# Mixture-of-experts block: expert outputs scattered into six planes, or added by the DMA into four

## The reference, cut to what matters

```
routing_weights = jax.nn.softmax(xf @ router_weight.T, axis=-1)
_, top_idx = jax.lax.top_k(routing_weights + e_score_bias, 6)
top_w = take(routing_weights, top_idx) / sum
combine = zeros((T, E)).at[arange(T)[:, None], top_idx].add(top_w)
gate, up = split(einsum('th,eih->tei', x, gate_up_proj), 2)
y = einsum('tei,ehi->teh', silu(gate) * up, down_proj)
out = einsum('teh,te->th', y, combine) + shared_out
x = x + gb * out
```

## Time and profile before

| | |
|---|---|
| median of 3 runs | 802.63 us (802.34 to 802.96) |
| span of the profiled execution | 799.6 us |
| time around the span, median less span | 3.0 us |
| expert loop, from the first gate matmul to the last down product | about 358 to 733 us |
| tail, from there to the end of the span | about 66 us |
| DMA traffic | 158.45 MB, 198 GB/s in the mean |

### The profile page before, as it was taken

The page is one execution under the profiler, slowest core; times in us unless marked ns, Lnnn a source line. Parts: engine busy times, 40 slices in busy tenths (PEclk is TensorE's granted clock), DMA queues, the critical chain, the costliest instruction groups (busy, mean ns, idle before and its releaser), DMA issues.

```text
span 799.6 us, 13266 instructions
## 1 busy us (share of the span) xinstructions
PE 740.7 (93%) x4302; PEld 590.7 (74%) x4302; DVE 480.8 (60%) x1207; ACT 400.0 (50%) x943; POOL 411.3 (51%) x420
## 2 busy tenths in 40 slices
PE   4989999999999898969999899999999999999963
PEld 4465667657657555549999799999999999997521
DVE  3676678879869954533555244444544544446986
ACT  5267574874464174115655455555565655662000
POOL 0000000267777777777777766765666666666000
PEclk9996999999999999989999999999999999999997
DMA  9420001024235896556676866765765666677995
GB/s 327 132 80 1 0 1 54 34 107 177 116 123 218 315 393 235 227 196 230 227 255 218 284 219 216 230 220 165 226 202 179 194 204 199 194 265 265 363 413 222
DMA packets 82605, 158.45 MB, mean 198 GB/s; under 512 B 14430, under 2 KB 55523, under 8 KB 82280
## 3 DMA queue, kind: packets, MB, share of 16 engines
q1 hardware_dynamic: 58344, 96.74, 36.9%
q0 software_dynamic: 19968, 56.67, 17.8%
q10 hardware_dynamic: 4224, 4.19, 1.5%
HBM read 88.15 MB, written 73.57 MB: 202 GB/s over the span
## 4 chain that ended last, share of the span: by engine, by line
PE 69%; DVE 9%; POOL 8%; DMA 5%; issue 4%; ACT 3%; SPq 2%; DVEq 0%; ACTq 0%; POOLq 0%
PE ps_wide L1320 17%; PE ps_wide L1335 12%; PE ps_kv L1320 8%; PE ps_wide L1089 8%; POOL expert_rows L541 8%; PE ps_narrow L1308 6%; DMA arena<-expert_outs 2%; PE ps_wide L1082 2%; PE ps_wide L1111 2%; PE ps_kv L1344 2%; PE ps_narrow L1040 1%; PE ps_narrow L1102 1%; PE ps_kv L1111 1%; DMA arena<-expert_rows 1%; DMA arena<-w_g 1%
## 5 line engine op out<-in xcount | busy, mean ns | idle before, releaser
L541 POOL DMA_INDIRECT expert_rows<-arena,slot_i x192 | 193.3, 1007 | 215.7 <-DVE arena L1638 151.2
L647 POOL DMA_INDIRECT expert_outs<-arena,meta x224 | 217.8, 972 | 111.7 <-DVE arena L1842 69.6
L894 ACT COPY arena<-arena 128x512 f32 x224 | 127.4, 616 | 157.0 <-PE ps_narrow L1308 153.4
L1842 DVE TENSOR_SCALAR arena<-ps_wide,meta 128x256 f32<-128x256 f32 x224 | 98.1, 479 | 129.9 <-PE ps_wide L1335 129.4
L1320 PEld LDWEIGHTS ps_wide<-arena 128*128 128x128 f32 x1200 | 148.4, 195 | 4.0 <-issue 0.2
L1320 PE MATMUL ps_wide<-arena 128*128 128x128 f32 x1200 | 149.0, 278 | 0.0
L1335 PE MATMUL ps_wide<-arena 128*128 x448 | 116.1, 382 | 0.9 <-DVE arena L1818 0.5
L1335 PEld LDWEIGHTS ps_wide<-arena 128*128 128x128 f32 x448 | 76.8, 191 | 7.4 <-issue 1.5
L1089 PE MATMUL ps_wide<-arena 128*128 128x512 f32 x168 | 75.4, 597 | 2.8 <-DVE arena L1532 2.8
L1308 PE MATMUL ps_narrow<-cst,arena 128*128 128x128 f32 x448 | 69.2, 277 | 7.9 <-DMA arena<-expert_rows 7.8
L1320 PEld LDWEIGHTS ps_kv<-arena 128*128 128x128 f32 x592 | 71.8, 192 | 1.9
(11 more groups left out here) (235 smaller groups left out, 1012.3 us busy)
## 6 DMA issues: line engine op xcount, KB each, us to landing
arena<-expert_rows SPq DMA_DIRECT2D x224, 160.0 KB, 2.8
arena<-expert_outs SPq DMA_DIRECT2D x48, 512.0 KB, 13.2
arena<-w_experts SPq DMA_DIRECT2D x32, 384.0 KB, 8.3
expert_rows<-pad_row SPq DMA_DIRECT2D x33, 160.0 KB, 5.0
out<-x ACTq DMA_DIRECT2D x8, 512.0 KB, 10.1
expert_outs<-arena,meta POOLq DMA_INDIRECT x224, 3.1
x<-x SPq DMA_DIRECT2D x3, 1024.0 KB, 11.1
h_cols<-arena SPq DMA_DIRECT2D x6, 512.0 KB, 3.8
```

Of the source, the lines that this page charges most:

```text
L541: nc.gpsimd.indirect_dma_start(rows, bass.IndirectOffsetOnAxis(ap=slots_i[b % 2][:, t, k:k + 1], axis=0), hrows[b % 2][:, t, :], None, bou ...
L647: nc.gpsimd.indirect_dma_start(outs, bass.IndirectOffsetOnAxis(ap=meta_i[:, j % METAS, 1:2], axis=0), yb[j % OUTS], None, bounds_check=las ...
L894: last = nc.scalar.copy(wgu[:, j % 4:j % 4 + 1, :], wall[:, bass.ds(expert[j], 1), 0:DOWN])
L1842: v.tensor_scalar(yb[j % OUTS], ps_wide[:, 1, p % 2, j % DUO * D:(j % DUO + 1) * D], meta[:, j % METAS, 0:1], None, ALU.mult).then_inc(s_y ...
```

## The change

`expert_outs` becomes four DRAM tensors (planes) of T + 128 rows. They are zeroed by four DMAs from the zero row early in the kernel. The store of block j adds its 128 rows to plane j % 4 (`compute_op=ALU.add`), and POOL issues it after the store of block j - 4, the one before it in the same plane, has landed. Padding rows now point to the 128 rows behind the T tokens and are stored too. `rows_of_slots` loses its scan; the output row is the token. The tail reads four planes a part into `FIN` = 6 sets, `CLEAR` is 5, PE and DVE share the planes anew, both wait for all four planes of a part, and SP no longer waits for the last (empty) blocks' stores before it loads the remaining parts.

```diff
-OUT_ROWS = TOPK * T
+PLANES = 4
+FIN = 6
+PLANE_ROWS = T + P
...
-FIN = 4
-BY_PE = [[3, 4, 5] if n in (3, 5, 7) else [4, 5] for n in range(8)]
-BY_DVE = [[k for k in range(TOPK) if k not in by_pe] for by_pe in BY_PE]
+BY_DVE = [[0, 1, 2] if n == 0 else [0] if n in (5, 7) else [0, 1] for n in range(8)]
+BY_PE = [[k for k in range(PLANES) if k not in by_dve] for by_dve in BY_DVE]
...
             sp.dma_start(rows[E * REGION:E * REGION + P, :], pad_row[:]).then_inc(s_stored, 16)
+            for q in range(PLANES):
+                sp.dma_start(outs[q].rearrange("(n p) d -> p n d", p=P),
+                             pad_row[:, None, 0:D].to_broadcast([P, PLANE_ROWS // P, D])).then_inc(s_zero, 16)
...
-                for k in BY_PE[n] + BY_DVE[n]:
-                    sp.dma_start(fin[n % FIN][k], outs[k * T + first:k * T + first + PART * P, :].rearrange(
-                        "(p t) d -> p t d", p=P)).then_inc(s_fin_pe[n] if k in BY_PE[n] else s_fin[n], 16)
+                for k in range(PLANES):
+                    sp.dma_start(fin[n % FIN][k], outs[k][first:first + PART * P, :].rearrange(
+                        "(p t) d -> p t d", p=P)).then_inc(s_fin[n], 16)
...
             for n in range(CLEAR):
                 load_planes(n)
-            for u in range(UNROLL):
-                sp.wait_ge(s_put[u], 16 * ROUNDS // LAPS)
             sp.wait_ge(s_y, DUOS)
             for n in range(CLEAR, PARTS):
                 load_planes(n)
+            for u in range(UNROLL):
+                sp.wait_ge(s_put[u], 16 * ROUNDS // LAPS)
...
+            pool.wait_ge(s_zero, 16 * PLANES)
             for j in range(BLOCKS):
                 u = j % UNROLL
+                if j >= PLANES:
+                    old = j - PLANES
+                    pool.wait_ge(s_put[old % UNROLL], (old // UNROLL + 1) * 16)
                 pool.wait_ge(s_yc, j + 1)
-                nc.gpsimd.indirect_dma_start(outs, bass.IndirectOffsetOnAxis(ap=meta_i[:, j % METAS, 1:2], axis=0),
-                                             yb[j % OUTS], None, bounds_check=last_out,
-                                             oob_is_err=False).then_inc(s_put[u], 16)
+                nc.gpsimd.indirect_dma_start(outs[j % PLANES], bass.IndirectOffsetOnAxis(ap=meta_i[:, j % METAS, 1:2], axis=0),
+                                             yb[j % OUTS], None, bounds_check=last_out, oob_is_err=True,
+                                             compute_op=ALU.add).then_inc(s_put[u], 16)
...
-                    link(v.tensor_tensor_scan(planes.rearrange("p t e -> p (t e)"), not_first.rearrange("p t e -> p (t e)"),
-                                              mask.rearrange("p t e -> p (t e)"), 0.0, ALU.mult, ALU.add))
-                    link(v.scalar_tensor_tensor(pairs.bitcast(U32)[:, :, :, 1], planes, float(T), tok[:, :, None].to_broadcast(wide),
-                                                ALU.mult, ALU.add))
+                    link(v.tensor_scalar(pairs.bitcast(U32)[:, :, :, 1], tok[:, :, None].to_broadcast(wide), 0.0, None, ALU.add))
```

More of the change, by code:

```diff
@@ L96, in adaln_block_kernel @@
         h2_cols = nc.dram_tensor("h2_cols", (PARTS - 2, P, C, HALF), F32, kind="Internal").ap()
-        outs = nc.dram_tensor("expert_outs", (OUT_ROWS, D), F32, kind="Internal").ap()
+        outs = [nc.dram_tensor(f"expert_outs{q}", (PLANE_ROWS, D), F32, kind="Internal").ap() for q in range(PLANES)]
         gate_rows = nc.dram_tensor("gate_rows", (1, B, 2, D), F32, kind="Internal").ap()
@@ L154, in adaln_block_kernel @@
         at[0] = 0
-        fin = [[take(PART, D) for _ in range(TOPK)] for _ in range(FIN)]
-        assert at[0] <= wall_end and CLEAR * PART * TOPK * D <= (E - 1) * WCOLS
+        fin = [[take(PART, D) for _ in range(PLANES)] for _ in range(FIN)]
+        assert at[0] <= wall_end and CLEAR * PART * PLANES * D <= (E - 1) * WCOLS
         at[0] = 0
@@ L226, in adaln_block_kernel @@
         counted_at = at[0]
-        mask, planes, not_first = (take(TILES, E) for _ in range(3))
+        mask = take(TILES, E)
+        take(2 * TILES, E)
         slot8 = take(TILES, 8)
@@ L338, in adaln_block_kernel @@
         s_fin = [sem(f"s_outputs_in{i}") for i in range(PARTS)]
-        s_fin_pe = [sem(f"s_outputs_in_for_tensor{i}") for i in range(PARTS)]
+        s_zero = sem("s_planes_zeroed")
         s_acc, s_read, s_res = sem("s_planes_summed"), sem("s_planes_read"), sem("s_result")
@@ L536, in _ @@
             last_row = nc.gpsimd.to_reg(E * REGION - 1)
-            last_out = nc.gpsimd.to_reg(OUT_ROWS - 1)
+            last_out = nc.gpsimd.to_reg(PLANE_ROWS - 1)
             def scatter_row(b, n):
@@ L1409, in sum_planes @@
                 shares = TAIL[n] in LAST
-                pe.wait_ge(s_fin_pe[n], 16 * len(BY_PE[n]))
+                pe.wait_ge(s_fin[n], 16 * PLANES)
                 for a in range(2):
@@ L1460, in _ @@
             v.memset(seen[:, 0, :], 0.0)
-            link(v.memset(not_first, 1.0))
-            v.memset(not_first[:, :, 0:1], 0.0)
             v.memset(score[:, :, E:E + 2], SENTINEL).then_inc(s_slot, 1)
@@ L1701, in body @@
                     v.tensor_scalar(pad_row[:, D:ROW].rearrange("p (e n) -> p e n", n=2).bitcast(U32)[:, :, 1],
-                                    pad_no.to_broadcast([P, E]), float(OUT_ROWS - T), None, ALU.add).then_inc(s_pad_row, 1)
+                                    pad_no.to_broadcast([P, E]), 0.0, None, ALU.add).then_inc(s_pad_row, 1)
                     for t in range(TILES):
-                        v.tensor_scalar(tok[:, t:t + 1], tok0[:, 0:1], float(PART), float(t // PART * PART * P + t % PART - T),
+                        v.tensor_scalar(tok[:, t:t + 1], tok0[:, 0:1], float(PART), float(t // PART * PART * P + t % PART),
                                         ALU.mult, ALU.add)
@@ L1886, in add_planes @@
             def add_planes(n):
-                dve.wait_ge(s_fin[n], 16 * len(BY_DVE[n]))
+                dve.wait_ge(s_fin[n], 16 * PLANES)
                 f = fin[n % FIN]
```

## The result

The changed kernel takes 872.79 us (median of 4 runs, 870.97 to 874.08) where the kernel before, run beside it, takes 802.80 (802.34 to 804.02): a ratio of 1.086 (95% interval 1.084 to 1.088). Forecast were 785 us and a range up to 815. It is 70 us slower, and the forecast is wrong in sign. The experiments ran in four groups, and in groups 1, 2 and 4 the kernel before took 890.7, 888.7 and 890.8 us but 803.9 in group 3, on the same chip as group 2 and for a reason that no record shows, so each ratio is to the kernel before of the same group.

What follows compares the result with a forecast made beforehand. PE was taken to bound the expert loop, DVE's adds and plane traffic the tail. 799.6 - 19.4 (tail) + 1.6 (loop) = 781.8, plus 3.0 around the span, gave about 785 us; own range 780 to 792, full range 779 to 815.

Steps and rivals of the forecast that it cites:

- POOL's own time: Loop: what an adding store costs POOL beyond a plain one, between 0 and 0.97 us; taken as 0.
- The first rival: Loop: POOL's descriptions become the bound; d us more a store eats the gain at d = 0.27; chance 0.18.
- its formula: Loop loss for d us more a store: 96d - 8.0 until block 95, 128 (d - 0.27) behind it.
- its cover: POOL's spare time in the loop: 8.0 us until block 95, 0.083 us a store; afterwards 0.27 a store.
- break-even: The extra POOL time per store, 0.27 us, at which the loop's loss eats the tail's gain of 19.4 us.
- The DMA engines' term: Loop: an addition takes 0.34 us more engine time; shares reach 0.85 and 0.90, under 1, so PE stays the bound.
- Landing: Loop: an adding store lands after about 4.5 us, bounds 3.1 and 5.9; in the last 25 us perhaps 9 or 10.
- The wait four back: Loop: POOL's new wait for the store four blocks earlier is over before POOL gets to it.
- Zeroing: Front: four DMAs, 17.3 MB, from about 38 us, ending between 98 and 163 us; cost 0.
- Tail: After the loop: DVE starts at 734.1 and part 7 closes at 776.9, a gain of 19.4 us.

Runs made afterwards that it cites:

- the dropped rows: The kernel before plus an indirect DMA, all its rows dropped, behind every second store: 1036.38 us, ratio 1.169; 148 us more where the formula gave 101.

## Why the prediction was wrong, step by step

**The step that failed** is *POOL's own time*: "What POOL needs to describe an addition is open: 0 at the least [...] 0.97 at the most [...] I take 0". The measured value is 0.569 us, a little above the middle of the two ends, and at that size POOL and not PE sets the pace of the loop. The reason given, that bytes do not count, is true and proves too little: it says what the time does not depend on (a scatter of longer rows takes the same), and nothing about another kind of operation. The Trainium skill, "GPSIMD Engine Reference", section "4. When to use GPSIMD", was named for the rival (one core writes the read descriptions, the other the write ones). The runs fit it in direction, but 1541 / 972 = 1.59 is neither 1 nor 2, and no run here looks at the two cores.

**The first rival named the mechanism, and its formula held for the loop.** 96 x 0.569 - 8.0 = 46.6 us until block 95, 128 x (0.569 - 0.27) = 38.3 behind it. The trace has 47.2 more from the first store to the last scatter (595.3 - 376.8 against 171.3) and 44.3 more from there to the last store, late landings among them. That 785 + 84.9 = 870 also meets the measured 872.8 and 870.0 is partly luck. DVE's tail starts 81.3 us later than before (815.4 against 734.1), 8.3 of it from the front, so the loop cost 73.0, fewer than the 86.5 of the formula and the forecast's 1.6 together, because the tail does not wait for the last stores. The tail gave 8.7 us (62.2 to 53.5) and not 19.4. The rival had 0.18; its cover (0.083 us a store until block 95) had been worked out rightly, and it should have weighed more: a term with no row, whose bounds are 0 and 0.97 us, against a cover of 0.08 and a break-even at 0.27. Taken flat between its ends, d lies above 0.27 in 0.72 of the cases.

**The DMA engines' term was mis-sized too**, without deciding. From the queue: 35.7% of 872.3 us is 311.4. I estimate the 192 scatters at the 0.34 us that a DMA of this queue had before, 65.3; the other 246.1 / 224 = 1.10 us is the engine time of an adding store. The same store without the addition: 19.5% of 778.8 = 151.9, less 65.3, 0.39 us. The addition costs 0.71 us, where I took 0.34; it is 2.8 times the plain store. The Trainium skill, "Collectives: The Full Stack", section "The bandwidth ceiling: the fold count and why AG ≠ RS ≠ AR", which would make it twice, is too low for these rows of 1 KB. If POOL were free, the engines would be next: from 550 to 640 us, where the kernel without the addition has a share of 0.66, 57 stores x 0.71 / 90 = 0.45 would come on top, more than 1. That is worked out and not shown by a run.

**What held.** Landing: 4.9 us, taken 4.5, bound 5.9; at most 9.2, taken 9 or 10. The wait four back: nothing (6 waits, 5.6 us in all, in the kernel without the addition, with a total as forecast). Zeroing: forecast to end between 98 and 163 us, and hidden; its four issues start at 38.6 to 61.5 us and land in 17.2 to 28.5 us, so by about 90 us, a little before the earlier bound, and runs of it alone cost nothing. Tail, in the kernel without the addition: the last L1899 of before (L1902 there) starts at 774.2, forecast "at about 777"; its first add is at 732.9. PE's and DVE's deals over eight parts, the plane loads and the moved wait all came out within 3 us together. **What showed only in part:** the tail's gain in the changed kernel itself. In group 3 DVE's tail takes 55.0 us with the addition and 42.5 without: beside POOL's last 14 stores the DMA engines are full (1.10 above) and a plane load lands after 21.8 us in the median, 13.5 without the addition. The prediction had put the traffic of these stores at nothing for the tail.

**The front.** Its first store is 8.3 us later than before in the first profile; in group 3 it is only 1.5 us later than in the kernel without the addition (372.0 to 370.5). In the first profile PE's granted clock was 0.54 from 190 to 200 us, where before had 1.00:

```profile
190.00:200.00 10.00, 10.00 (x43) 8.45 (x42) 5.76 (x19) 1.43 (x2) 4.85 (x5) 0.54 0.31 125
```

That is the lower of its two levels (1.2 and 2.4 GHz) for most of the stretch. The same kernel in group 3 had 1.00 in that stretch, so neither the zeroing nor the missing scan brings it each time. Why it fell in that execution no run settles; it is worth a few microseconds of 70.

**Open:** the 47 us too many of the dropped rows.

## What to carry to other kernels

When an engine that only issues transfers is back to back in a stretch, work out its cover per instruction, and price every change in the kind of its instruction as if it were compute: here 0.57 us by 224 stores broke a cover of 0.08. When a term has no row, ask at which value the sign turns and how much of the bounded interval lies beyond it, before choosing an end of it. Traffic saved in a tail can be paid for many times over in the loop that prepares it, if it is bought with an operation per block.

## What the runs showed of the hardware

- An indirect store of 128 rows takes POOL 0.972 us, an adding one 1.541, whether a row has 512 bytes or 1 KB, and one whose rows are all dropped 0.976; that one still puts 48 packets into the queue ((25344 - 19968) / 112).
- A DMA that adds takes 144 packets where the plain one takes 48 ((41472 - 19968) / 224 = 96 more), and 1.10 us of engine time instead of 0.39; with half the bytes 0.74 (25.7% of 903.4 us, less 65.3, by 224). A straight line through the two, an estimate, leaves 0.39 of the 1.10 that does not go away with the bytes.
- The bytes in the queue's row (60.84 MB with and without the addition) don't contain what the addition reads, nor do the 79.76 MB of HBM reads on the page, which are the same in both kernels: its cost shows in packets and in the engines' share alone, as in the loop at 0.89 of the engines for 168 GB/s.
- An adding store lands after 4.9 us, a plain one after 3.4 into the same planes (medians); beside the plane loads the adding ones took 7.7 to 9.2.
